# First experts in whole float32, sixteen experts over groups of 1024 tokens, outputs up to four experts behind

## The reference

```python
t = t + _L1_ffn_ref(_ln_t(t), gate_w, gate_b, w1, w2, w3)

logits = x @ gate_w + gate_b            # 16 experts
probs = softmax(logits)                 # two largest kept, divided by their sum
dispatch = one_hot(top_idx) * top_probs
h1 = einsum('bsd,edh->bseh', x, w1)     # d 64, e 16, h 128
h2 = einsum('bsd,edh->bseh', x, w2)
hidden = silu(h1) * h2
expert_out = einsum('bseh,eho->bseo', hidden, w3)
return einsum('bseo,bse->bso', expert_out, dispatch)
```

## Time and profile before

| | |
|---|---|
| three runs | 663.58, 664.87, 670.53 us; median 664.87 |
| profiled execution | 661.8 us, span 660.1, mean granted clock 0.938 |
| PE busy | 581.5 us (88%) |
| DVE, ACT, POOL busy | 427.1, 328.7, 300.9 us |
| first experts, first silu to last output | 157.0 to 363.1 us |
| second experts, first gelu to last | 445.5 to 568.3 us |

### The profile page before, as it was taken

One profiled execution on the slowest core, in us unless ns is written; L12 is line 12 of the kernel. 1 busy time (PEld: TensorE's weight loads), 2 busy tenths in 40 slices (PEclk: granted clock), 3 DMA queues, 4 the chain that ended last, 5 costly groups with the idle time before them and its releaser, 6 DMA issues.

```text
span 660.1 us, 11021 instructions
## 1 busy us (share of the span) xinstructions
PE 581.5 (88%) x3576; PEld 353.4 (54%) x3576; DVE 427.1 (65%) x1249; ACT 328.7 (50%) x625; POOL 300.9 (46%) x375
## 2 busy tenths in 40 slices
PE   7888894876999999989989797998999999997883
PEld 6675433775455555555554657993333333367642
DVE  6654598688887877758768847644963333435557
ACT  3334695185444444344344645545555555336384
POOL 6501746150235448667684970360434242435153
PEclk9997896597999999999999998999999999997796
DMA  4810000020723522432240100033522222000001
GB/s 117 147 29 1 2 0 1 12 53 23 174 67 74 126 65 65 111 81 64 65 113 15 33 0 1 2 62 86 114 65 65 64 65 64 1 2 1 1 2 65
DMA packets 27029, 34.62 MB, mean 52 GB/s; under 512 B 11304, under 2 KB 20544, under 8 KB 24992
## 3 DMA queue, kind: packets, MB, share of 16 engines
q1 hardware_dynamic: 26976, 33.95, 22.6%
HBM read 32.50 MB, written 1.44 MB: 51 GB/s over the span
## 4 chain that ended last, share of the span: by engine, by line
PE 61%; DVE 19%; POOL 10%; ACT 5%; issue 5%; DVEq 0%; POOLq 0%; ACTq 0%
PE ps L1834 13%; PE ps L2535 9%; PE ps L2525 9%; PE ps L1878 6%; POOL out_acc L1487 4%; DVE ST L489 3%; PE ps L423 3%; POOL dw_out L1600 3%; PE ps L2635 2%; POOL tap_prod L1610 2%; PE ps L766 1%; PE ps L2944 1%; DVE tk L1092 1%; PE ps L2214 1%; PE ps L2228 1%
## 5 line engine op out<-in xcount | busy, mean ns | idle before, releaser
L1487 POOL TENSOR_TENSOR out_acc<-out_acc,tok_tmp 128x512 f32<-128x512 f32 x84 | 109.9, 1308 | 190.0 <-DVE tok_tmp L2421 88.6
L1834 PE MATMUL ps<-tokT,w 128*128 128x512 f32 x512 | 135.7, 410 | 4.8 <-ACT act_buf L1793 2.7
L1793 ACT ACTIVATE act_buf<-ps 128x512 f32<-128x512 f32 x128 | 75.4, 597 | 98.0 <-PE ps L1834 93.7
L1834 PEld LDWEIGHTS ps<-tokT,w 128*128 128x128 f32 x512 | 92.1, 190 | 54.5 <-issue 24.3
L2525 PE MATMUL ps<-tokP,w 64*128 64x512 f32 x256 | 63.8, 616 | 0.1
L1731 DVE TENSOR_TENSOR hid_four<-act_buf,ps 128x512 f32<-128x512 f32 x64 | 43.3, 684 | 21.1 <-ACT act_buf L1793 17.3
L1731 DVE TENSOR_TENSOR tok_split<-act_buf,ps 128x512 f32<-128x512 f32 x64 | 43.0, 684 | 18.2 <-ACT act_buf L1793 17.2
L534 ACT ACTIVATE U<-X,nmr,rstd 128x64 f32<-128x64 f32 x120 | 41.8, 429 | 22.1 <-POOL nmr L512 17.8
L2421 DVE SCALAR_TENSOR_TENSOR tok_tmp<-ps,b,disp_all 128x512 f32<-128x512 f32 x28 | 21.0, 751 | 46.4 <-PE ps L2535 39.0
L2480 ACT ACTIVATE hid_four<-ps,b 128x1024 f32<-128x1024 f32 x32 | 33.9, 1111 | 29.8 <-PE ps L2525 29.8
L2480 ACT ACTIVATE tok_split<-ps,b 128x1024 f32<-128x1024 f32 x32 | 33.9, 1110 | 25.4 <-PE ps L2525 25.4
(11 more groups left out here) (482 smaller groups left out, 1036.5 us busy)
## 6 DMA issues: line engine op xcount, KB each, us to landing
disp_all<-disp_dram SPq DMA_DIRECT2D x44, 512.0 KB, 6.3
w_raw<-in_L_ffn_w SPq DMA_DIRECT2D x4, 512.0 KB, 9.2
disp_all<-disp_dram SPq DMA_DIRECT2D x4, 384.0 KB, 5.2
XIN<-in_x SPq DMA_DIRECT2D x4, 256.0 KB, 3.6
w_raw<-in_L_ffn_W SPq DMA_DIRECT2D x2, 512.0 KB, 6.1
out<-XIN SPq DMA_DIRECT2D x4, 256.0 KB, 2.8
fc_raw<-in_L_conv_upfc_w SPq DMA_DIRECT2D x1, 512.0 KB, 4.7
w<-in_L_ffn_w SPq DMA_DIRECT2D x1, 512.0 KB, 9.2
```

The lines of the kernel that those rows point to most:

```text
L1487: pool.tensor_tensor(out_acc[:, :], out_acc[:, :], weighed[p % 2], ALU.add).then_inc(mm["acc"].sem, 1)
L1793: act.activation(act_buf[e % 2][:, :], ps[:, e % 2, :], ACT.Silu).then_inc(mm["act"].sem, 1)
L1834: last = pe.matmul(ps[:, 2 * k + e % 2, :], w12[:, part, k, EXPERT1[e], :], tokT[:, bass.ts(i, CHUNK)], start=(part == 0), stop=(part == 1))
```

## The change

- The split of tokens, gate weights and w1, w2 is gone. tokP (four transposes a group) replaces tokT. Between the groups PE now has eight filling matmuls (keep_clock) each time, where it had eight, three, three, three.
- The experts run over groups of 1024 tokens: 64 rounds in place of 128. A round is: first product (two matmuls, banks 0 and 1), outputs of the expert two before (two matmuls), second product (two matmuls, banks 2 and 3). One silu and one gate over 1024 columns; one weighing and one addition a round, 15 additions a group.
- In the first group, the first two experts' products and gates stand within the first half's top-2, and the outputs of the first experts come later (E1_FIRST_OUT), up to four behind.
- out_acc is double. Walk-back, sum and norm of a group stand in rounds 3 to 11 of the next; the norm is still made by chunks, so two chunks are left for the end of the last group. POOL's steps of the convolution stand one behind most additions, from round 13 of groups 1 and 2 to round 12 of the next.
- Dispatch rows are stored by group with four DMAs (pair_store) and loaded four experts at a time; the loads are as many and as large as before.

```diff
@@ -215,16 +215,15 @@
...
-        w12 = sb("w12", [P, 2, 2, E1, H1], F32R, region="gated")
+        act_pair = [sb(f"act_pair{i}", [P, 2 * CHUNK], region="gated") for i in range(2)]
...
-        out_acc = sb("out_acc", [P, CHUNK], region="mid")
+        out_acc = [sb(f"out_acc{i}", [P, CHUNK], region="mid") for i in range(2)]
...
@@ -1447,33 +1426,32 @@
...
+        def pair_store(sp, mm, ne, rows, half, groups, at, stored):
+            sp.wait_ge(*mm["dt"](half))
+            for g in groups:
+                lane, col = at(g)
+                for i in range(4):
+                    part = lane + i * 2 * ne
+                    sp.dma_start(rows[g].rearrange("(e r i s) -> i r e s", e=ne, r=2, i=4)[i],
+                                 disp_rows[part:part + 2 * ne, col:col + P]).then_inc(stored, 16)
+            sp.wait_ge(stored, 64 * (groups[-1] + 1))
...
+        def pair_load(sp, mm, ne, rows, n, landed):
+            g, q = n // (ne // 4), n % (ne // 4)
+            k = n % 2
+            rows = rows[g].rearrange("(e r s) -> r e s", e=ne, r=2)
+            if n >= 2:
+                sp.wait_ge(*mm["w"](2 + 4 * (n - 1)))
+            alone = 1 if n == 0 else 0
+            if alone:
                 for r in range(2):
-                    src = dram[i, r * 2 * pairs + k * pairs + alone:r * 2 * pairs + (k + 1) * pairs, :]
-                    sp.dma_start(disp_all[r * C:(r + 1) * C, k, alone:pairs, :],
-                                 src.unsqueeze(0).to_broadcast([C, pairs - alone, CHUNK])).then_inc(landed[k], 16)
+                    sp.dma_start(disp_all[half(r), 0, 0:1, :],
+                                 rows[r, 0:1, :].unsqueeze(0).to_broadcast([C, 1, CHUNK])).then_inc(landed[2], 16)
+            for r in range(2):
+                sp.dma_start(disp_all[half(r), k, alone:4, :],
+                             rows[r, 4 * q + alone:4 * q + 4, :].unsqueeze(0).to_broadcast([C, 4 - alone, CHUNK])).then_inc(landed[k], 16)
...
@@ -1534,54 +1510,40 @@
...
+            def between(i, e):
+                if i >= 1 and e in (5, 7):
+                    chunk_rstd(pool, 2 * i - 2 + (e == 7), eps_c, m["d_var"], m["d_rstd"])
+                for g, n in dw_steps(i, e):
+                    dw_pool(pool, g, n)
+            add_weighed(pool, e1, E1, between, count=G)
...
-            chunk_rstd(pool, NCHUNK - 1, eps_c, m["d_var"], m["d_rstd"])
+            for i in (NCHUNK - 2, NCHUNK - 1):
+                chunk_rstd(pool, i, eps_c, m["d_var"], m["d_rstd"])
...
+        DW_STEPS, DW_FROM = 17, 13
+        DW_SLOTS = DW_FROM - 1 + E1 - DW_FROM
+        def dw_steps(i, e):
+            g, slot = (i - 1, e - DW_FROM) if e >= DW_FROM else (i - 2, e - 1 + E1 - DW_FROM)
+            if not 0 <= g < G - 2:
...
+            first, end = [-(-DW_STEPS * x // DW_SLOTS) for x in (slot, slot + 1)]
+            return [(g, n) for n in range(first, end)]
...
@@ -1615,27 +1577,15 @@
...
+        def experts_finish(dve, mm, g):
+            xs = X[:, g * TG:(g + 1) * TG, :]
+            dve.wait_ge(*mm["t_ps"](g + 2))
+            dve.tensor_tensor(xs, xs, ps[:, 7, :].rearrange("p (t c) -> p t c", c=C), ALU.add).then_inc(mm["ta"].sem, 1)
+            dve.wait_ge(*mm["ta"](g + 2))
...
@@ -1701,76 +1651,76 @@
...
+        E1_FIRST_OUT = {2: (0,), 3: (1,), 6: (2,), 7: (3,), 8: (4, 5), 9: (6, 7)}
+        E1_FIRST_W = {6: (0, 1), 7: (2,), 8: (3, 4, 5), 9: (6, 7)}
...
+            def gate(i, e):
+                n = i * E1 + e
+                dve.wait_ge(*mm["act"](n + 2))
+                dve.wait_ge(*mm["h2_ps"](n + 1))
+                dve.wait_ge(*mm["o_ps"](n + 1))
+                dve.tensor_tensor(hid_pair[n % 4], act_pair[n % 2][:, :], ps[:, 2:4, :].rearrange("p r s -> p (r s)"),
+                                  ALU.mult).then_inc(mm["m1"].sem, 1)
...
+            def group(i, prev):
+                for e in range(2 if prev is None else 0, E1):
+                    if prev is not None and e == 4:
+                        experts_finish(dve, mm, prev)
+                    if prev is None and e < 10:
+                        for x in E1_FIRST_W.get(e, ()):
+                            weigh(i, x)
+                    elif e >= 2:
+                        weigh(i, e - 2)
+                    else:
+                        weigh(prev, E1 - 2 + e)
+                    gate(i, e)
+                    if prev is None:
+                        if e >= 4:
+                            router_top2(dve, mm, route1, 1, E1, e - 4)
+                        if e >= 11:
+                            for t in range(2 * (e - 11), min(2 * (e - 11) + 2, 9)):
+                                dw_place(dve, t)
+                        continue
+                    for step in {4: (0, 1, 2, 3), 5: (4, 5), 6: (0, 1, 2, 3), 7: (4, 5)}.get(e, ()):
+                        chunk_stats(dve, 2 * prev + (e >= 6), X, m["d_var"], step)
+                    if prev == 0 and e == 11:
+                        prep_gates(dve)
             router_logits(dve, mm, route1, 0, E1, b_gw[:, :], 6)
+            router_logits(dve, mm, route1, 1, E1, b_gw[:, :], 7)
             for step in range(5):
                 router_top2(dve, mm, route1, 0, E1, step)
-            router_logits(dve, mm, route1, 1, E1, b_gw[:, :], 7)
-            for step in range(5, TOP2_STEPS):
+            gate(0, 0)
+            for step in range(5, 9):
                 router_top2(dve, mm, route1, 0, E1, step)
...
+            gate(0, 1)
+            for step in range(9, TOP2_STEPS):
+                router_top2(dve, mm, route1, 0, E1, step)
+            group(0, None)
...
-            for p in (PAIRS1 - 2, PAIRS1 - 1):
-                weigh(NCHUNK - 1, p)
+            for e in (E1 - 2, E1 - 1):
+                weigh(G - 1, e)
...
-            for step in range(STEPS):
-                chunk_stats(dve, NCHUNK - 1, X, m["d_var"], step)
+            experts_finish(dve, mm, G - 1)
+            for i in (NCHUNK - 2, NCHUNK - 1):
+                for step in range(STEPS):
+                    chunk_stats(dve, i, X, m["d_var"], step)
...
@@ -1779,38 +1729,50 @@
...
+            def group(i, prev):
                 for e in range(E1):
...
+                    n = i * E1 + e
+                    act.wait_ge(*mm["h_ps"](n + 1))
+                    if n >= 2:
+                        act.wait_ge(*mm["m1"](n))
+                    act.activation(act_pair[n % 2][:, :], ps[:, 0:2, :].rearrange("p r s -> p (r s)"), ACT.Silu).then_inc(mm["act"].sem, 1)
                     if prev is None:
...
+                        if e == 2:
+                            router_move(act, mm, 0, 6)
+                        if e == 15:
+                            router_move(act, mm, 1, 6)
+                        continue
+                    if e in (9, 11):
+                        chunk_norm(act, 2 * prev + (e == 11), m["d_rstd"], m["d_u"])
+                    if e == 14:
+                        d_padded(act, prev)
...
@@ -1818,66 +1780,74 @@
...
-                router_tensor(pe, g, gw2, E1, 6, mm["lg_ps"])
...
+                pe.wait_ge(*mm["ft"](g + 1))
+                for i in range(4):
+                    n, at = 4 * g + i, (4 * g + i) % 8 * 2 * E1
+                    last = pe.matmul(ps[:, 6 + g // 2, at:at + 2 * E1], tokP[:, n * P:(n + 1) * P],
+                                     gw_both[:, :, :].rearrange("p r e -> p (r e)"), start=True, stop=True)
+                last.then_inc(mm["lg_ps"].sem, 1)
...
+            for g in range(G):
+                tr(g)
+                keep_clock(pe, 3, 8)
+                if g >= 1:
+                    logits(g - 1)
+            logits(G - 1)
...
+            def first(i, e):
+                n = i * E1 + e
+                pe.wait_ge(*mm["act"](n + 1))
+                for r in range(2):
+                    last = pe.matmul(ps[:, r, :], w12_raw[half(r), 0, e, :], tokP[half(r), i * CHUNK:(i + 1) * CHUNK], start=True, stop=True)
+                last.then_inc(mm["h_ps"].sem, 1)
...
+            def second(i, e):
+                n = i * E1 + e
+                pe.wait_ge(*mm["m1"](n + 1))
+                for r in range(2):
+                    last = pe.matmul(ps[:, 2 + r, :], w12_raw[half(r), 1, e, :], tokP[half(r), i * CHUNK:(i + 1) * CHUNK],
+                                     start=True, stop=True)
+                last.then_inc(mm["h2_ps"].sem, 1)
+            def group(i, prev):
                 for e in range(E1):
...
+                    first(i, e)
+                    if prev is None and e < 10:
+                        for x in E1_FIRST_OUT.get(e, ()):
+                            e1_outp(pe, i, x)
+                        if e == 2:
+                            router_transpose(pe, mm, route1, 0, (6, 6))
+                    elif e >= 2:
+                        e1_outp(pe, i, e - 2)
+                    elif prev is not None:
+                        e1_outp(pe, prev, E1 - 2 + e)
+                    second(i, e)
```

(28 more changed lines are left out.)

316 lines of the change are left out of this document (61 added, 255 removed).

## The result

| | before | after |
|---|---|---|
| median of the runs, us | 666.83 (663.58 to 670.53, 4 runs) | 653.74 (653.08 to 655.11, 4 runs) |
| profiled execution, us | 661.8, span 660.1 | 653.08, span 651.3 |
| ratio after to before | | 0.9848, 95% interval 0.9804 to 0.9893 |

The changed kernel is 1.5% faster, and the interval lies clear of 1. Against the forecast of 656 the median is 2.3 us lower, inside the range; between the profiled executions the step is -8.7 us where the sum said -9.0. Between the medians it is -13.1 us, and the traces show only the 8.7 of it: the profiled execution of the kernel before lies 5.0 us under its median, that of the changed kernel 0.7 under its own. The total is right, but its terms are not: the front gave 3.5 us and not 0, the tail took 4.4 and not 1.7, and the steady part gave 9.6 and not 10.7.

A forecast was written before the change was run, and what follows sets the result against it. TensorE sets the pace, waiting on a chain through GpSimd's additions, silu and gate. Steady part -10.7, front 0, tail +1.7 sum to -9.0 us: 652.8 against the profiled 661.8, 655.9 as median, forecast 656, range 649 to 665.

The forecast's parts named there:

- the front: Front and routing, up to group 1: no net gain, 0, with -3 and +4 us as ends.
- the tail: After the last output: a second chunk norm in GpSimd's tap chain adds 1.7 us, with +1 and +4 as ends.
- the steady part: Chunk 2's first product to the last output block: 10.7 us gained, as stops go and TensorE's work stays nearly equal.
- Work of a round: TensorE's six matmuls and two switches take 2.92 us a round; against the split form a draw, 140.2 against 139.0 us.
- Stops of the kernel before: TensorE, chunk 2 to last output: 157.8 us hold 146.4 of work and 11.4 of stops, which go.
- New stops: Steady part of the changed kernel: 1 us left for new waits, with 0.5 us slack behind the gate.
- Sets: TensorE's sets of transposes for walk-backs and the next layer: 0.5 us each, 3.0 us for six after the change.
- (a): Rival, gate as the bound: a gate of 2.1 us under GpSimd's additions costs 17 us, 673; chance 0.11.
- (b): Rival, single PSUM banks: waiting for the own bank makes a round 4.25 us, 64 us more, 720; chance 0.01.
- (c): Rival, the start goes wrong: serial routing, half clock to about 165, +4 to +6, 660 to 662; chance 0.12.
- (d): Rival, GpSimd falls behind: backlog over 3.8, stops stay at 6 to 8 us, 661 to 664; chance 0.11.
- (e): Rival, no loss at all: the start gives 3, nothing stops, 650 to 652; chance 0.1.

The follow-up runs named there:

- b_both: Kernel before, with the walk-back one expert later and the chunk norm moved behind the second silu of the chunk after next: 659.91 us, ratio 0.9884.
- b_norm: Kernel before, with a chunk's norm on ScalarE moved from the last silu of the next chunk to the second silu of the chunk after: 665.11 us, ratio 1.000.
- a_fills: Changed kernel with 16 idle matmuls before the third group's keys, where TensorE waits for GpSimd's taps: 653.15 us, ratio to the kernel before 0.9803.
- a_gate_2: Changed kernel with two extra VectorE instructions, results unused, ahead of the gate in every round: 689.65 us, ratio to the kernel before 1.0396.
- a_combined: Changed kernel with 3 idle matmuls for 8 behind the last three token transposes, one norm for the last two chunks, seven taps before the third group's keys: 650.06 us.
- a_taps: Changed kernel with TensorE's last five taps of the fourth group issued before the third group's keys instead of behind its values: 654.56 us, ratio to kernel before 0.9841.
- a_norm8: Changed kernel with one GpSimd norm for the last group's two chunks in place of two: 657.82 us, ratio to the kernel before 0.9862.

## Why the prediction was right, and where it was not

- **Work of a round: right.** 2.92 us forecast, 2.93 measured; 48 of them 140.4 (2.925 each). Eight whole matmuls and the doubled switches cost what the earlier trace rows gave. The claimed draw is confirmed by b_both and b_norm (147.0 and 146.9 us of work in split form, 148.2 now).
- **Stops of the kernel before: right.** 157.8 less 146.4 of work is 11.4, and 5.5 of it could be taken out of the kernel before by two changes of order.
- **New stops: 1 us forecast, 0 measured.** Gate 1.22 (1.23), silu 1.02 (1.11); slack behind the gate 0.42 (0.5). The backlog on GpSimd was never waited for.
- **Sets: mis-sized.** 0.5 us was read from the second experts; here one costs 0.78, six of them 4.7 and not 3.0. That is 1.7 us more, of which the stop that did not come gives 1 back: most of the difference between -9.6 and -10.7.
- **Front, "0": wrong, -3.5.** Three steps failed. "The sixteen splits of the weights lie beside VectorE's top-k loop: 0": two of them lay beside instructions of VectorE on the path, 1.2 (0.7 in b_norm). "The split on VectorE goes, but it was not what came last": before, TensorE's last stop was for one (1.58 us at 142.34); with the doubled fills giving part back, 0.9. And the routing came out 1.1 shorter, a microsecond of which had been set aside for the clock. The steps of the routing themselves held: last logits to first silu 3.3 us forecast (150.6 to 153.9), 3.2 measured (148.0 to 151.22); the transposed weights at 158.31, 2.6 earlier than said, as the logits. The remaining 0.4 is open.
- **Tail, "+1.7": the mechanism right, the sum wrong, +4.4.** The second norm is 1.84 on the tap chain: taps take 26.31 to 26.39 us in the five executions that left this stretch and the gate as they were, 24.47 to 24.50 in the four with the old code, whatever the clock. The other 2.6 are what the longer pause brought in its wake: the half clock from 374.9 to 381.7. In a_fills, without it, keys to context take as long as before. The prediction had the pause grow by 1.7 (it grew by 2.9) and asked nothing of the clock behind it, although had a stretch at 0.77 behind such a pause.
- **Rivals.** (a) did not occur, and a_gate_2 shows its price; (b) did not: TensorE is busy 148.20 of 148.20 us with one pair of banks for each product, so the rule to rotate through PSUM banks (the Trainium skill, "Perfetto Trace Analysis", Optimizing Tensor Performance (Matmuls)) bought nothing where other banks' matmuls fill the wait. (c) half clock ended at 156.5, not past 162. (d) no wait for GpSimd. (e) came closest in the steady part and the front; the tail kept it from being the total.

The forecast of 656 was hit within 0.4% by luck: a front that was 3.5 us too pessimistic met a tail that was 2.7 and a steady part that was 1.1 too optimistic. The 2.3 us that are left are not in the sum (-9.0 against -8.7) but in the 3 us that the forecast put between profiled execution and median, where the changed kernel has 0.7.

## What to carry over

Where one engine is the bound and its list of instructions is fixed, count its work first and the stops second: here a change of number format drew, and the schedule that came with it paid the 9.6 us of the steady part. Moving one wait out of such a list shows the next one (b_norm: 3.8 us of waits went, 5.1 came), so look who is late then. A stop of the matrix engine that grows should be priced with the clock behind it, and filling it with real work looks worth more than idle matmuls: at an equal half clock of 10.2 us, taps and rest of attention are 81.2 us in a_combined and 83.5 in a_fills, of which 0.4 is the norm. That is one execution each, and a_taps alone gained nothing that its total shows.

## What the runs showed of the hardware

The granted clock is half not only behind pauses. In a_norm8 TensorE was busy without a gap from 412 to 434 us and had the clock of 1.2 GHz for the last ten:

```profile
412.00:420.00 8.00, 8.00 (x70) 7.76 (x69) 7.62 (x45) 4.34 (x11) 5.96 (x10) 1.00 0.01 3
420.00:424.00 4.00, 4.00 (x36) 3.82 (x35) 2.33 (x13) 2.82 (x8) 3.52 (x8) 0.99 0.18 44
424.00:434.00 10.00, 10.00 (x50) 10.00 (x49) 0.54 (x4) 3.00 (x5) 4.94 (x5) 0.50 0.45 84
```

The matmuls ahead of it were short ones: biases with one column, idle ones, transposes. The changed kernel ran the same instructions at 1.00 there (423.00 to 434.00 above). The Trainium skill, "TensorE: Matmul & The Clock Gate", Part 1, ties the half clock to a TensorE that was idle a while ago; by its busy time this row differs. What decides stays open. It costs: over the fourteen profiled executions the attention behind the taps takes 54.2 to 57.1 us with 6.8 to 13.7 us of half clock, 56.9 and 59.1 in the two with 17, and 60.7 to 61.8 in the four with 20.5.
